# Two stages rescheduled: weight splits in pieces in the experts layer, keys by quarters in differential attention

## What is computed

```python
logits = xf @ router_w + router_b
topk_vals, topk_idx = jax.lax.top_k(logits, 2)
gates = softmax(sparse)                                   # 8 routed experts
routed = vmap(lambda w1, w3, w2: silu(xf @ w1) * (xf @ w3) @ w2)(routed_w1, routed_w3, routed_w2)
out = einsum('etd,te->td', routed, gates) + shared experts (2 of them, same form, gate 1)
```

```python
q = (x @ Wq.T) -> [token, 32 heads, 16] * 16**-0.5;  k the same way, unscaled;  v -> [token, 16 heads, 32]
att = softmax(nan_to_num(einsum('bnqd,bnkd->bnqk', q, k)))           # 32 x 32 for each token
lam = exp(sum(lq1 * lk1)) - exp(sum(lq2 * lk2)) + LAMBDA_INIT
att2 = att[first 16 queries, first 16 keys] - lam * att[last 16, last 16]
out = rmsnorm(einsum('bnah,bhnd->bnad', att2, v)) * (1 - LAMBDA_INIT);  return out @ Wo.T + bo
```

## Time and profile before

| | us |
|---|---|
| median of 3 runs | 3347.14 (3340.43 to 3347.51) |
| the profiled execution | 3343.08 |
| its span, first to last instruction | 3341.3 |
| experts stage, in it | 651 to 1007 |
| differential attention: projections; attention | 2727 to 2801; 2801 to 2914 |

### The profile page before, as it was taken

How to read it: one execution, slowest core, us unless ns; L and a number is a source line. 1 busy time by engine, 2 the same in 40 slices (tenths; PEclk the granted TensorE clock), 3 DMA queues, 4 the chain that set the end, 5 groups by cost and what they waited for, 6 DMA issues and landing times. The chain is left out here.

```text
span 3341.3 us, 55974 instructions
## 1 busy us (share of the span) xinstructions
PE 2923.3 (87%) x23532; PEld 2286.5 (68%) x23532; DVE 1652.9 (49%) x3398; ACT 1126.0 (34%) x1791; POOL 83.2 (2%) x68
## 2 busy tenths in 40 slices
PE   5997878699997999999999999999999856679755
PEld 3443666577776888888888888888888645558622
DVE  5223432434344545554555555554555455654586
ACT  2212122222123433443433344443344311523384
POOL 0001000100000000000000000000000100030000
PEclk9998999799998999999999999999999878789867
DMA  6885010111104110111111011111011029111200
GB/s 233 301 272 199 26 42 0 54 38 50 44 19 130 33 41 21 35 43 43 43 31 33 24 43 43 43 33 41 21 35 46 17 78 129 32 48 44 97 24 25
DMA packets 169236, 213.67 MB, mean 64 GB/s; under 512 B 51120, under 2 KB 120752, under 8 KB 168128
## 3 DMA queue, kind: packets, MB, share of 16 engines
q1 hardware_dynamic: 148320, 206.39, 20.4%
q10 hardware_dynamic: 20704, 4.20, 0.9%
HBM read 197.97 MB, written 10.49 MB: 62 GB/s over the span
## 5 line engine op out<-in xcount | busy, mean ns | idle before, releaser
L69 PE MATMUL xa_J<-xa_c_hi,xa_wk_hi 128*128 128x402 f32 x1024 | 367.7, 359 | 5.9 <-DVE xa_c_lo L84 5.9
L1438 DVE CUSTOM_DVE_ANT_0 xa_pr<-xa_S,xa_m 128x402 f32<-128x402 f32 x512 | 270.9, 571 | 170.7 <-PE xa_S L1592 170.7
L71 PE MATMUL xa_J<-xa_c_hi,xa_wk_lo 128*128 128x402 f32 x1024 | 354.5, 346 | 0.0
L70 PE MATMUL xa_J<-xa_c_lo,xa_wk_hi 128*128 128x402 f32 x1024 | 354.4, 346 | 0.0
L69 PE MATMUL xa_J<-xa_wv_hi,xa_c_hi 128*128 128x512 f32 (+1 forms) x832 | 345.8, 416 | 0.0
L70 PE MATMUL xa_J<-xa_wv_lo,xa_c_hi 128*128 128x512 f32 (+1 forms) x832 | 327.5, 394 | 0.0
L71 PE MATMUL xa_J<-xa_wv_hi,xa_c_lo 128*128 128x512 f32 (+1 forms) x832 | 327.3, 393 | 0.0
L1328 ACT ACTIVATE xa_kT<-xa_J,cl_bk 128x402 f32<-128x402 f32 x256 | 151.8, 593 | 325.9 <-PE xa_J L71 278.5
L1465 DVE TENSOR_TENSOR cl_v<-xa_J,cl_bv 128x512 f32<-128x512 f32 (+1 forms) x208 | 142.2, 690 | 225.1 <-PE xa_J L71 180.0
L1347 ACT ACTIVATE xa_pT<-xa_T 128x512 f32<-128x512 f32 (+1 forms) x256 | 138.9, 543 | 337.3 <-PE xa_T L1608 337.3
L1473 DVE COPY xa_pT<-xa_T 128x512 f32<-128x512 f32 x192 | 132.6, 691 | 234.7 <-PE xa_T L1608 234.7
(11 more groups left out here) (394 smaller groups left out, 4965.6 us busy)
## 6 DMA issues: line engine op xcount, KB each, us to landing
bs_rows<-in_ctx SPq DMA_DIRECT2D x48, 1024.0 KB, 7.6
main_x<-in_ctx_cols SPq DMA_DIRECT2D x192, 201.0 KB, 3.0
bs_cols<-in_ctx_cols SPq DMA_DIRECT2D x24, 802.0 KB, 8.6
main_x<-in_ctx_cols SPq DMA_DIRECT2D x64, 197.5 KB, 3.3
moe_raw<-in_L_ffn_routed_w SPq DMA_DIRECT2D x24, 512.0 KB, 4.2
diff_raw<-in_L_attn_W SPq DMA_DIRECT2D x16, 512.0 KB, 3.4
bs_cols<-in_ctx_cols SPq DMA_DIRECT2D x8, 796.0 KB, 6.0
bidaf_w_raw<-in_L_xattn_W_qv SPq DMA_DIRECT2D x4, 1024.0 KB, 9.2
```

Source lines behind the costliest of these rows:

```text
L69: pe.matmul(out, w_hi, x_hi, start=first, stop=False)
L70: pe.matmul(out, w_hi, x_lo, start=False, stop=False)
L71: return pe.matmul(out, w_lo, x_hi, start=False, stop=last)
L1438: nc.vector.tensor_tensor_reduce(out=pr[:, r, ks], in0=S[:, r, 0:KG], in1=m[:, ks], scale=1.0, scalar=NEVER, op0=ALU.add, op1=ALU.max, acc ...
```

## The change

Experts: the split of the next expert's `raw13` is cut up. ScalarE does it in two instructions (w1, w3), VectorE in four (half of w1, half of w1, half of w3, half of w3), and VectorE does one of the four ahead of each of the additions t = 1 to 4 instead of all ahead of t = 0. The semaphores count 2 and 4 per expert.

Projections of the differential layer: VectorE does the lambda arithmetic here; its first two steps at the stage's start, behind a wait for the lambda loads, the rest ahead of the fifth tile's scaling. ScalarE does the small exp here. The first keys are loaded in 32 DMAs, a quarter of the size each.

Attention: GpSimd clears nothing; ScalarE clears the two halves of `B`, one ahead of exp(0) and one behind it. Keys are loaded, waited for and replaced by quarters: the tokens are put in another order (`group`), so that a quarter of a round's keys is one stretch of `K`, free again when that quarter's scores are made. SP loads the second round's first quarter ahead of the second values. The result's hi and lo splits write the tokens back in their true order, in runs of 32 elements.

```diff
@@ experts_stage
-                    sp.wait_ge(w13_lo_ready, n)
+                    sp.wait_ge(w13_lo_ready, n * 4)
...
-                    split_hi(nc, w13_hi[:], raw13[:]).then_inc(w13_hi_ready, 1)
+                    for j in range(2):
+                        split_hi(nc, w13_hi[:, j], raw13[:, j]).then_inc(w13_hi_ready, 1)
...
-                def split13(n):
-                    dve.wait_ge(w13_hi_ready, n + 1)
-                    split_lo(nc, w13_lo[:], raw13[:], w13_hi[:]).then_inc(w13_lo_ready, 1)
+                def split13(n, i):
+                    dve.wait_ge(w13_hi_ready, 2 * n + i // 2 + 1)
+                    j, ks = i // 2, slice(2 * (i % 2), 2 * (i % 2) + 2)
+                    split_lo(nc, w13_lo[:, j, ks], raw13[:, j, ks], w13_hi[:, j, ks]).then_inc(w13_lo_ready, 1)
...
-                    if more:
-                        split13(n + 1)
                     dve.wait_ge(gate_ready, n + 1)
                     for t in range(TILES):
+                        if more and 1 <= t <= 4:
+                            split13(n + 1, t - 1)
                         dve.wait_ge(o_produced, TILES * n + t + 1)
...
-                    pe.wait_ge(w13_lo_ready, n + 1)
+                    pe.wait_ge(w13_lo_ready, n * 4 + 4)
@@ DiffInputs
-    def load_keys(self, engine, r):
-        src = self.k.rearrange("(r x s) (d j) -> r s d x j", r=ROUNDS, s=8, d=QD)
+    def load_keys(self, engine, r, e):
+        src = self.k.rearrange("(r e x s) (d j) -> r e s d x j", r=ROUNDS, e=QUARTERS, s=8, d=QD)
         for s in range(8):
-            engine.dma_start(self.K[QD * s:QD * s + QD, s % 4, :, :], src[r, s]).then_inc(self.k_loaded, 16)
+            engine.dma_start(self.K[QD * s:QD * s + QD, s % 4, 16 * e:16 * e + 16, :], src[r, e, s]).then_inc(self.k_loaded[e], 16)
+    def group(self, r, e, c, g):
+        return (((r * QUARTERS + e) * COLS) + c) * SETS + g
@@ differential_inputs_stage, ScalarE
                 split_hi(nc, w_hi[:, 1, :, :], raw[:, 1, :, :]).then_inc(w_hi_ready, 1)
+                act.wait_ge(lam_summed, 1)
+                nc.scalar.activation(lam_exp[:], lam_sum[:], ACT.Exp).then_inc(lam_exp_ready, 1)
...
-                ins.load_keys(act, 0)
+                for e in range(QUARTERS):
+                    ins.load_keys(act, 0, e)
@@ differential_inputs_stage, VectorE (after the four lo splits of the first weights)
+                dve.wait_ge(ins.lam_loaded, 64)
+                pairs = ins.lam_in[:].rearrange("p (a b) d -> p a b d", b=2)
+                link(nc.vector.tensor_tensor(lam_prod[:], pairs[:, :, 0, :], pairs[:, :, 1, :], ALU.mult))
+                nc.vector.reduce_sum(lam_sum[:], lam_prod[:], AX.X).then_inc(lam_summed, 1)
...
+                        if n == 4:
+                            head_weights()      # the seven instructions removed below
@@ differential_stage, SP
                 ins.double_values(sp, 0)
+                ins.half_stored(sp, 1, 1)
                 ins.half_stored(sp, 2, 1)
+                sp.wait_ge(scored, 1)
+                ins.load_keys(sp, 1, 0)
                 ins.load_values(sp, 1)
-                ins.half_stored(sp, 1, 1)
-                sp.wait_ge(scored, QUARTERS)
-                ins.load_keys(sp, 1)
+                for e in range(1, QUARTERS):
+                    sp.wait_ge(scored, e + 1)
+                    ins.load_keys(sp, 1, e)
                 ins.double_values(sp, 1)
-            @block.gpsimd
-            def _(pool):
-                nc.gpsimd.memset(B[:], 0.0).then_inc(b_cleared, 1)
@@ differential_stage, PE
-                        pe.wait_ge(ins.k_loaded, 16 * ins.K_DMAS * (r + 1))
+                    pe.wait_ge(ins.k_loaded[quarter], 16 * ins.K_DMAS * (r + 1))
@@ differential_stage, ScalarE
+                def clear(i):
+                    whole = B[:, i].rearrange("p n c s w a -> p (n c s w a)")
+                    nc.scalar.activation(whole, ident[:, 0:1].to_broadcast([P, BLOCKS * COLS * P]), ACT.Copy, scale=0.0).then_inc(b_cleared, 1)
-                act.wait_ge(lam_summed, 1)
-                nc.scalar.activation(lam_exp[:], lam_sum[:], ACT.Exp).then_inc(lam_exp_ready, 1)
-                act.wait_ge(b_cleared, 1)
+                clear(0)
                 exp(0)
+                clear(1)
+                act.wait_ge(b_cleared, 2)
@@ differential_stage, VectorE: removed ahead of front(0)
-                dve.wait_ge(ins.lam_loaded, 64)
-                link(nc.vector.tensor_tensor(lam_prod[:], ...
-                nc.vector.reduce_sum(lam_sum[:], lam_prod[:], AX.X).then_inc(lam_summed, 1)
-                nc.vector.tensor_reduce(which[:], ident[:].rearrange("p (c d) -> p c d", c=COLS), AX.X, ALU.add)
-                link(nc.vector.tensor_reduce(side[:], ident[:].rearrange("p (c w a) -> p w c a", c=COLS, w=2), AX.XY, ALU.add))
-                dve.wait_ge(lam_exp_ready, 1)
-                link(nc.vector.tensor_tensor(lam[:], lam_exp[:, 0:1], lam_exp[:, 1:2], ALU.subtract))
-                link(nc.vector.tensor_scalar(lam[:], lam[:], LAMBDA_INIT, None, ALU.add))
-                link(nc.vector.tensor_scalar(wm[:], side[:], lam[:, 0:1], None, ALU.mult))
-                nc.vector.tensor_copy(wm[:, 0:1], side[:, 0:1])
-                link(nc.vector.tensor_scalar(wm[:, 1:2], wm[:, 1:2], -1.0, None, ALU.mult))
```

59 lines of the change are left out of this document (37 added, 22 removed).

## The result

The changed kernel takes 3319.18 us (median of 4 runs, 3317.82 to 3321.28), beside 3346.31 us for the kernel before on the same chip (4 runs, 3340.43 to 3347.51). The ratio is 0.9924, with a 95% interval of 0.9909 to 0.9940. A second series of five runs on another chip gave 0.9929 (0.9915 to 0.9942). The profiled execution of after lies on a span of 3318.2 us where before's is 3341.3, so 23.1 us are there to be found in the two traces.

A forecast was written before the change was run, and what follows sets the result against it. TensorE was taken to bound the experts, VectorE attention. Experts 14.3 plus attention 13.4 (5.9 + 8.0 - 0.5) make 27.7 us, giving 3315.4 or 3319.4 by starting time; middle 3317.5, 8-in-10 range 3309 to 3330.

The forecast's parts named there:

- Experts: Experts stage: nine TensorE stalls behind VectorE's additions go, 14.0 us; with smaller terms 14.3, between 13.3 and 14.6.
- Projections: Projections of the differential layer: moving the lambda arithmetic there costs nothing, upper bound 0.5 us; stage as long as before (74 us).
- The pieces' price: Experts, VectorE: one quarter of the lo split costs 0.7 us, bounds 0.57 and 0.75.
- TensorE's slack: Experts: each addition ends 1.6 us or more before TensorE wants it.
- Rival (a): Experts: pieces late or dearer, so the stall only moves; half of the 14 us stays, 3325 us; chance 0.07.
- Start of attention: Attention: front(0) starts at 2802.7 instead of 2808.64, a gain of 5.9 us, with ScalarE's two clearings (3.6 us each) hidden.
- Rival (d): Attention: quarters bring nothing, front(4) waiting for something else, or the clearing is not hidden; 8 us lost, 3326; chance 0.07.
- Keys by quarters: Attention, second round: earlier keys remove 8.0 of 8.75 us of waiting at front(4) and front(5), between 5.7 and 8.75.
- the landing: Attention, SP's key loads: landing trails the last issue by 5.3 us as before, so quarter 1 lands at 2837.4.
- My own sign of being wrong: Attention, SP's queue: the forecast is wrong if issues of small DMAs take over 0.7 us.
- half clock: Attention, TensorE: 0.6 us lost in each step at 1.2 GHz, up to 3 over the round; taken as 0.5 us.
- Rival (b): Attention: TensorE at half clock becomes the bound, or the second quarter comes late; 6 us lost, 3324; chance 0.10.

The follow-up runs named there:

- the repeat: The changed kernel timed once more, unaltered, on another chip beside the variants: 3317.85 us (5 runs, 3317.34 to 3320.41), ratio 0.9929 against the kernel before.

## Why the prediction was right, and where it was not

The forecast of 3317.5 us stands beside 3319.18 measured, and the mechanism, experts first and attention second, is the one that the runs show. But the sum of 27.7 us is made of terms that missed in both directions: experts 15.7 instead of 14.3, attention 9.0 instead of 13.4, together 24.7. That the time lies within 1.7 us of the forecast is partly luck: the medians of the first series differ by 27.1 us, those of the second by 23.8 (3341.69 and 3317.85), and the first holds a kernel before that was some 3 us slower than in the other series.

**Experts: mechanism right, term too small.** I put a stall at 1.55 us, the start-to-start time of its first matmul less the usual 0.23. It was 1.69 by the period. The step that failed is that I let the stall end with its first matmul; that one ran 0.50 us and the next started 0.33 us behind it instead of 0.23, so the matmuls behind a stall are slow for a moment and belong to its price. 9 x 0.14 = 1.3 us. The first expert's gain was 0.64 us (4.28 to 3.64 from hi split to first matmul) instead of 0.3, since four pieces in a row took 2.50 and not 2.8 us; one alone takes 0.68. The pieces' price beside additions (0.68), TensorE's slack and the windows 33.5 apart (33.3) held; the register arithmetic took 37 ns in its rows on SP's queue, as before. Rival (a) is out.

**Start of attention: size right, worth wrong.** 5.8 us against 5.9, the clearing at 3.6 us each, both hidden, all as forecast. What failed is the addition. I added 5.9 and 8.0 as two faults apart; the kernels with the memset alone, with lambda alone and with whole keys show that an earlier start alone only makes the wait of front(4) longer. The queue in the earlier trace rows had said it: it is paced by its transfers, so it doesn't move with front(0). The same holds for my sentence that dropping the memset alone would bring nearly the whole gain: it is right for the instruction (0.23 us) and wrong for the time (3345.40). Rival (d) in the form "front(4) waits for something else" did come in part: front(4) waited 2.06 us for a stop of TensorE, and with fronts 5 and 7 it is 4.8 us instead of 8.

**Keys by quarters: right that they pay, price and landing wrong.** I took 8.0 of 8.75 us. The second round gained 3.5 us on its own measure. Two steps failed. The first is the price: I took a quarter at 12.73 / 4 = 3.2 us, and quarter 0 took 8.50 and quarter 1 8.02 (2817.14 to 2825.16), together 10.1 us more than the 6.4 of my sum. Even my bound for a fixed price, 8 x 0.66 = 5.3, was too low, because I used the shortest issue as the price of one; on a full queue the mean decides, and 8.50 / 8 = 1.06 and 0.83 us lie between the shortest and the median in the earlier trace rows (0.66 and 1.42). Values took 9.90 instead of 12.50. The second step is the landing: I let it trail the last issue by 5.3 us as before, and for quarter 1 it trailed by 1.5 (2825.16 to 2826.70). These two, 2.6 and 3.7 us, gave more than half of it back, so quarter 1 released its scores at 39.4 instead of 34.7 us behind front(0), and front(5) waited 1.10 (in the repeat 1.52). scores(6) started 1.10 us late for its quarter, but no front waited for it. My own sign of being wrong, small issues on SP of over 0.7 us, did come; that the time stayed in the range is owed to the shorter landing, the faster values and the experts.

**TensorE: not the clock but the instructions.** I had 0.5 us for half clock. The runs show 2.06 + 1.66 us of waiting at front(4) and front(7) for stops in the instruction stream, which no rival named. Rival (b) had the place right (TensorE late in attention) and the cause wrong; the run without second loads has slow matmuls and no wait. The releaser "issue" alone doesn't tell such a stop from a wait for a DMA: the earlier trace rows shows scores(4) of before released by "issue" after 9.47 us, and there my reading as keys was right. The last key issue started at 2838.17, and its landing row (DMA view of before in the window 2838.16 to 2838.9: queue, KB each, us to landing) puts its end at 2844.0, just ahead of the 2844.09 at which scores(4) began:

```profile
di_K<-diff_k SPq DMA_DIRECT2D x1, 128.0 KB, 5.8
```

In the four other kernels with whole keys scores(4) also start 0.09 us behind the last landing.

**Projections: right.** The 32 key issues on ScalarE's queue took 17.02 us instead of 9.52, and the values' loads still start with their stores; lambda's later instructions lie in the gap named in the earlier trace rows (timeline of after, ACT's queue and DVE):

```profile
2754.79 17.02 ACTq L1791 DMA_DIRECT2D di_K<-diff_k  x32
...
2776.47 8.83 ACTq L1797 DMA_DIRECT2D di_V<-diff_v  x4
...
2731.63 0.23 DVE L1902 TENSOR_SCALAR di_wm<-pd_side,pd_lam 128x2 f32<-128x2 f32 x1
...
2732.92 0.69 DVE L1920 TENSOR_SCALAR pd_kept<-pd_out 128x512 f32<-128x512 f32 x1 [0.68 <-PE pd_out L71]
```

The scaling behind lambda's last instruction still waits 0.68 us for TensorE, of the 2.03 that were free: hidden. The first two steps were later than I said: VectorE waited for the lambda loads until 2723.94, and the second weight split moved by 1.3 us (12.57 instead of 11.28 behind the clearing of `K`), not 0.2 to 0.8. The four banks covered it: the stage is as long as before. The result's splits in runs of 32 elements cost nothing either, 2.07 us for four hi splits against 2.06.

**What stays open.** That the stops are late fetches of TensorE's instructions rests on four things that the traces show. They stand at fixed places of TensorE's program: in kernels with after's program behind 51 matmuls of scores(4), 98 of weigh(1), 16 of weigh(2), 16 of scores(6) and 62 of scores(7), which by the rows' counts is every 126 to 128 matmuls (the last step is two of them); in before's program behind 99 of weigh(1) and 18 of scores(6), again two such steps apart. Their length follows the transfers: 4.92 us to none in scores(4), 4.01 to none in scores(7), and without the second round's loads one of 1.30 is all that is left. The third is the packets of the instruction queue. The DMA view of after in the window 2842 to 2844 and the page's DMA part (queue, kind: packets, MB, share of 16 engines) have these rows:

```profile
q1 hardware_dynamic: 31, 0.25, 90.0%
q8 instruction: 1, 0.02, 2.8%
...
q8 instruction: 164, 2.69, 0.3%
```

## What to carry to other kernels

Before adding two gains in one stage, ask what fixes the start of the work behind the first: if a queue that doesn't depend on it does, the first is worth nothing until the second is made. When DMAs are cut, price a piece by the mean of a full queue, not by the shortest issue, and count what stands behind the pieces in the same queue: here the second cut, from 32 to 16 KB, lost nearly as much by the doubling that it pushed back (6.8 us) as by the keys themselves (7.9). A stop in the middle of a run of equal matmuls that the trace releases by "issue" was neither clock nor data here; see whether it comes again at the same matmul, and whether a packet of the instruction queue ends shortly ahead of its end, before tuning the order of the loads. Ahead of a group, "issue" can be a DMA's landing.

## What the runs showed of the hardware

- A GpSimd memset that only writes SBUF held an SBUF-to-SBUF `tensor_scalar` of 128x2 (4.97 us, without it 0.23) and of 128x32 (1.80 us) until its own end. Instructions reading PSUM, a reduction and a `tensor_scalar` of 128x1 (0.15 us) ran through.
- An issue of keys on SP's queue took, in the mean of its group, 0.61 to 0.79 us for 16 KB, 0.74 to 1.06 for 32 KB, 0.76 for 96 KB and 1.59 to 1.85 for 128 KB.
- The last key landed 1.5 us behind the end of its issue in quarters of 32 KB pieces (quarter 1 of after), and 5.2 us behind it in whole loads of 128 KB (before).
- TensorE stopped in the middle of groups of equal matmuls, at places 126 to 128 matmuls apart, for up to 4.9 us beside heavy transfers and for at most 1.3 us without them. Each stop ended 1.2 to 2.0 us behind the end of a 16 KB packet of the instruction queue. The waits of VectorE that this makes are worth about 4 us here and move when transfers move, which makes the last microseconds of this stage hard to tune.
- A stall on TensorE whose row says 1.39 us cost 1.69 us of the period; the first matmul behind it ran 0.50 us and the next started 0.33 us later, where 0.23 is usual.
